# Half of the tokens runs four expert entries ahead of the other half, in all four layers

## The chip, the cores and the metric

The kernel runs on one core of one Trainium2 chip. The metric is the device time of one launch in microseconds (us); each kernel is judged by the median of its runs. Before the change the three runs took 655.57, 655.82 and 659.88 us.

## What is computed

Four layers, each of them an attention block and a mixture of experts, on 1024 tokens (4 batches of 256) of width 128, all in float32. Every block works on a layer-normed x, and its result is added to x with a gate of its own:

```python
x = x + tanh(g_xattn[L]) * attention_L(layernorm(x), ctx_1024)
x = x + tanh(g_ffn[L])   * experts_L(layernorm(x))
```

The attentions have 16 heads of 8. Layer 0 weighs rolled values by the top lags of a correlation taken over the head's 8 positions, layer 1 is plain softmax attention with biases, layer 2 a band of 32 positions to each side with one key head for all queries, layer 3 softmax attention under a 256 x 256 mask, with biases. The experts:

```python
# layer 0: 32 experts silu(x@g)*(x@u)@d of width 64 and 8 "zero" experts (x itself); softmax + bias, top 6
# layer 1: 16 of the same form, top 2 renormed, and one shared expert of width 352 with a sigmoid gate
# layer 2: 31 experts gelu(x@W1+B1)@W2+B2 of width 128, top 3; one shared expert; and + x
# layer 3:  8 experts relu(x@W1+b1)@W2+b2 of width 256, top 2
out = sum_e gate[token, e] * expert_e(x)
```

## The kernel before

All tokens stay in SBUF. Every large product is made of three TensorE matmuls, high x high, high x low and low x high parts of fp32r numbers (`product`, L731 to L736), on 128 rows and 512 columns, so the 1024 tokens are two halves of 512 (`hf` 0 and 1).

*Experts.* Every token goes through every expert, weighted by its gate, which is zero where the expert wasn't chosen. An entry is a 128-wide piece of expert weights: 16 entries in layer 0 (two experts of width 64 side by side), 11 in layer 1 (8 such pairs and 3 pieces of the shared expert), 32 in layer 2, 16 in layer 3. A *unit* is an entry on one half of the tokens, so a layer has twice as many units as entries; unit u is entry u // 2 on half u % 2. A unit runs through the engines like this:

- SyncE loads the entry's weights into one of four ring slots (`fill_ring` L357 before the stage, `load_ring` L364 in it) and, from the fourth entry on, the entry's row of gates, broadcast to 128 partitions, into `gate_slot` (held in `qst`).
- GpSimd splits the weights into high and low parts (`split_weights` L467: L475 gives the high part, L477 the low one; `hidden_part` L480 for the up weights, `result_part` L486 for the down weights), once an entry.
- TensorE makes the up product (L738; three matmuls in the MLP layers 2 and 3, six in the GLU layers 0 and 1), for the first three entries spreads the gate row itself (L754), and makes the down product (L768), which adds to a sum that stays in PSUM, one bank a half, for the whole stage. The up of a unit stands two units ahead of its down.
- ScalarE applies silu, gelu or relu (`unit` L1168) and later copies the weighted result to `hid_hi` (`first_part` L1178).
- VectorE multiplies with the gate (L1589; in GLU layers gate by up first, L1575) and subtracts for the low part `hid_lo` (L1595). In layers 0 and 2 it also adds the layer's own input, tile by tile (`add_input` L1552).

*Start of a stage.* `ln_turned` (DVE, L1369; L1374 is the low part `xlo` of the turned, normed tokens) ends a norm. Half 0's is done first; then come the norm of half 1 and `route` (PE L703, DVE L1476, ACT L1147), whose operations take all eight tiles of 128 tokens at once: scores, top k, renorm, and a three-way bf16 split of the table, which TensorE turns into rows (`turn_rows` L715, `turn_weights` L721). Only then do units' products with gates begin.

*End of a stage.* The two sums are scaled (ACT and DVE), turned back by eight transposes (L829), added to x, and the next norm and the attention's query product (`project_queries` L853, weights split at `split_query_weights` L509) follow. In these stretches TensorE multiplies zeros (`keep_busy` L569, L572) where it would idle.

*Attention.* A hand-written software pipeline over (batch, head) steps p (`loop` L1024 and L1239; `window_loop` L1051 for layer 2): maxima, scores, exponentials on ScalarE (L1273), values, norm of the outputs, with the second half's queries projected at steps `Q_AT`. Layer 3 makes 16 mask products (L848) ahead of the loop.

Each engine runs its own instruction list in the order that the code writes; semaphores join them. No planner is involved.

## Time and profile before

| | |
|---|---|
| median of three runs | 655.82 us |
| the profiled execution | 655.92 us, of which the span of the trace is 654.1 us |
| mean granted TensorE clock | 0.967 |
| TensorE matmul busy | 594.5 us (91%), 3429 instructions |
| VectorE busy | 502.1 us (77%) |
| ScalarE busy | 360.2 us (55%) |
| GpSimd busy | 222.0 us (34%) |
| layer 3's mask products (L848) | 4.1 us for 16 matmuls, which the trace shows as 32 records |
| expert stages, from half 0's `xlo` to the last down | about 41 to 135, 228 to 294, 364 to 472, 583 to 643 us |

A page of the profile has its times in us. Engines are PE (TensorE), PEld (its weight loads), DVE (VectorE), ACT (ScalarE), POOL (GpSimd) and SP (SyncE, SPq its DMA issues). A matmul record is the time from its start to the end that is modelled for it; the next one starts before it ends, so a row of 0.39 us and the next start 0.23 us later go together. "[idle before <-X]" is the idle time ahead of an instruction and who ended it. PEclk is the granted clock as a share of full speed.

### The profile page before, as it was taken

Reading aid. Unit: us, or ns where it says so; the run is one execution under the profiler, and the core shown is the slowest. Engines: PE = TensorE matmul, PEld = TensorE weight load, DVE = VectorE, ACT = ScalarE, POOL = GpSimd, SP = SyncE. Lnnn points to the kernel's source line nnn. Section 1 sums busy time; section 2 is a strip of 40 time slices with the busy share of each in tenths; the row PEclk is TensorE's granted clock in tenths of the full one; section 3 lists DMA queues with packets and bytes.
Section 4 is the critical chain, followed back from the end, with each engine's and each line's share of the span. In section 5 each row is a group of like instructions: output and inputs, shape, how many; then the busy total and the mean of one; then the engine's idle time right before and its main releaser. Section 6 shows DMA issues by size and latency. Waiting matters only on the chain.

```text
span 654.1 us, 11738 instructions
## 1 busy us (share of the span) xinstructions
PE 594.5 (91%) x3429; PEld 433.6 (66%) x3429; DVE 502.1 (77%) x1287; ACT 360.2 (55%) x639; POOL 222.0 (34%) x438
## 2 busy tenths in 40 slices
PE   8898699978999878997999799999998999987996
PEld 6684588746776555874666556888865777754784
DVE  7857779978777357997753579999968888655996
ACT  6326345525666514553566157888824666632885
POOL 4211255432000212532112126888831000201783
PEclk9989889998999979999999899999997999998999
DMA  8225886210000005811000217777410000000771
GB/s 289 66 97 152 181 196 176 76 50 1 4 28 3 27 1 122 195 35 33 4 6 18 57 50 251 237 241 234 153 33 2 3 28 3 4 2 10 263 243 42
DMA packets 33134, 59.06 MB, mean 90 GB/s; under 512 B 6530, under 2 KB 22562, under 8 KB 33084
## 3 DMA queue, kind: packets, MB, share of 16 engines
q1 hardware_dynamic: 32508, 57.43, 30.1%
q10 hardware_dynamic: 576, 1.02, 0.4%
q8 instruction: 25, 0.41, 0.2%
q14 instruction: 25, 0.20, 0.1%
HBM read 53.61 MB, written 4.29 MB: 89 GB/s over the span
## 4 chain that ended last, share of the span: by engine, by line
PE 69%; DVE 16%; ACT 5%; issue 5%; SPq 3%; DMA 2%; POOL 1%; DVEq 0%; ACTq 0%
PE PS L734 11%; PE PS L736 10%; PE PS L735 10%; PE PS L983 5%; PE PS L891 4%; PE PS L966 4%; PE PS L572 2%; PE PS L963 2%; PE PS L1000 2%; DVE hid_lo L1595 2%; ACT pT L1273 2%; PE PS L939 1%; DVE qst L1649 1%; DVE PS L1589 1%; PE PS L920 1%
## 5 line engine op out<-in xcount | busy, mean ns | idle before, releaser
L475 POOL TENSOR_TENSOR wpair<-ring,ones_col 128x128 fp32r<-128x128 f32 (+1 forms) x150 | 80.0, 533 | 149.0 <-PE PS L736 125.0
L1273 ACT ACTIVATE pT<-PS 128x512 f32<-128x512 f32 x160 | 92.6, 595 | 46.0 <-PE PS L966 37.6
L1595 DVE TENSOR_TENSOR hid_lo<-PS,hid_hi 128x512 fp32r<-128x512 f32 x150 | 102.4, 682 | 1.8 <-ACT hid_hi L1182 1.3
L1182 ACT ACTIVATE hid_hi<-PS 128x512 fp32r<-128x512 f32 x150 | 88.9, 593 | 19.0 <-DVE PS L1589 18.5
L477 POOL TENSOR_TENSOR wpair<-ring,wpair 128x128 fp32r<-128x128 f32 (+1 forms) x150 | 93.2, 621 | 11.8
L734 PE MATMUL PS<-xhi,wpair 128*128 128x512 f32 x204 | 85.0, 417 | 6.0 <-POOL wpair L477 4.9
L735 PE MATMUL PS<-xlo,wpair 128*128 128x512 f32 x204 | 82.5, 404 | 0.0
L736 PE MATMUL PS<-xhi,wpair 128*128 128x512 f32 x204 | 82.3, 404 | 0.0
L1176 ACT ACTIVATE pT<-PS,ring 128x512 f32<-128x512 f32 x96 | 65.9, 689 | 17.6 <-PE PS L736 16.3
L734 PE MATMUL PS<-hid_hi,wpair 128*128 128x512 f32 x150 | 62.1, 414 | 6.8 <-DVE hid_lo L1595 6.4
L966 PE MATMUL PS<-qst,kz 128*128 128x256 f32 x256 | 64.6, 338 | 3.0 <-ACT pT L1273 3.0
L1589 DVE TENSOR_TENSOR PS<-pT,qst 128x512 f32<-128x512 f32 x84 | 62.8, 748 | 5.3 <-ACT pT L1176 2.3
L891 PE MATMUL PS<-kz,qst 128*128 128x256 f32 x256 | 60.6, 321 | 4.8 <-DVE negmax L1696 2.6
L532 POOL CAST nmpart<-negmax 128x8 fp32r<-128x8 f32 x48 | 9.1, 189 | 157.7 <-DVE emask L1703 67.3
L1696 DVE CUSTOM_DVE_ANT_0 consts<-PS,ctx_tok,negfloor 128x256 bf16<-128x256 f32 x128 | 54.6, 481 | 8.1 <-PE PS L891 7.8
L736 PE MATMUL PS<-hid_hi,wpair 128*128 128x512 f32 x150 | 58.9, 393 | 0.0
L735 PE MATMUL PS<-hid_lo,wpair 128*128 128x512 f32 x150 | 58.9, 393 | 0.0
L1176 ACT ACTIVATE pT<-PS 128x512 f32<-128x512 f32 x54 | 32.1, 598 | 48.4 <-PE PS L736 48.3
L1690 DVE TENSOR_REDUCE negmax<-PS 128x2 f32<-128x512 f32 x64 | 42.0, 688 | 15.8 <-PE PS L891 15.7
L891 PEld LDWEIGHTS PS<-kz,qst 128*128 128x128 f32 x256 | 40.5, 197 | 17.9 <-issue 6.9
L734 PEld LDWEIGHTS PS<-xhi,wpair 128*128 128x128 f32 x204 | 40.2, 197 | 16.9 <-POOL wpair L477 5.3
L966 PEld LDWEIGHTS PS<-qst,kz 128*128 128x128 f32 x256 | 45.6, 196 | 7.3 <-issue 2.8
(239 smaller groups left out, 1118.0 us busy)
## 6 DMA issues: line engine op xcount, KB each, us to landing
qst<-gates SPq DMA_DIRECT2D x42, 512.0 KB, 4.8
qst<-gates SPq DMA_DIRECT2D x42, 256.0 KB, 4.3
ring<-in_mlp SPq DMA_DIRECT2D x48, 128.5 KB, 3.3
ring<-in_glu SPq DMA_DIRECT2D x27, 192.0 KB, 4.6
kz<-keys SPq DMA_DIRECT2D x36, 96.0 KB
keys<-qst SPq DMA_DIRECT2D x6, 512.0 KB, 3.6
qst<-kfull SPq DMA_DIRECT2D x96, 4.0 KB
wq<-in_wq SPq DMA_DIRECT2D x3, 256.0 KB, 3.6
```

The lines of the kernel that those rows point to most:

```text
L475: pool.tensor_tensor(wpair[:, pair, 0, c], w, ones, ALU.mult).then_inc(M["wstep"], 1)
L477: pool.tensor_tensor(wpair[:, pair, 1, c], ring[:, slot, c], wpair[:, pair, 0, c].bitcast(f32), ALU.subtract).then_inc(ready, 1)
L734: pe.matmul(o, w_hi, hi, start=start, stop=False, skip_group_check=True)
L735: pe.matmul(o, w_hi, lo, start=False, stop=False, skip_group_check=True)
L736: return pe.matmul(o, w_lo, hi, start=False, stop=start, skip_group_check=True)
L891: mm = pe.matmul(PS[:, v % 2, q * S:(q + 1) * S], qst[:, h // HGRP, b * S + q * P:b * S + (q + 1) * P], keys_of(b, h), start=True, stop=True)
L966: mm = pe.matmul(PS[:, 2 + w % 2, k * S:(k + 1) * S], keys_of(b, h)[:, k * P:(k + 1) * P], qst[:, h // HGRP, b * S:(b + 1) * S], start=(L ...
L1176: act.activation(act_out[:, hf if glu else kept, :], PS[:, 2 + hf, :], func, bias=bias).then_inc(M["act"], 1)
L1182: act.activation(hid_hi[:, kept, :], PS[:, gate_bank(glu, kept), :], ACT.Copy).then_inc(M["hi"], 1)
L1273: act.activation(pT[:, w % 8, :], PS[:, 2 + w % 2, :], ACT.Exp, scale=sc).then_inc(A["p"], 1)
L1589: dve.tensor_tensor(o, src, row, ALU.mult).then_inc(M["hid"], 1)
L1595: dve.tensor_tensor(hid_lo[:, kept, :], PS[:, gate_bank(glu, kept), :], hid_hi[:, kept, :].bitcast(f32), ALU.subtract).then_inc(M["lo"], 1)
```

## The change

1. *Order of the units.* Half 0 runs four entries ahead: the first four units are entries 0 to 3 of half 0, then the halves alternate, half 1 four entries behind, and the last four units are half 1 alone. For these last four, entries 0 to 3 are read from memory and split a second time. "Step" s is an entry as it is loaded: s runs to n + 3, and s >= n are the second readings. An up now stands up to four units ahead of its down in layers 2 and 3.
2. *Routing.* Each half is scored and routed by itself; half 0's at the start of the stage, half 1's add, norm and routing between units 0 to 5. The table is turned as one f32 matrix, and its rows are kept as a high and a low part (`high_rows`, `low_rows`) with K = 64 in place of three bf16 parts with K = 96. Rows are saved and loaded from entry 6 on (unit 8).
3. *Ends.* Half 0's sum is complete four units before the end; it is turned back, added and normed between the last units, so attention begins with half 0's queries right behind the last down. The next layer's query weights are split in four pieces at steps 9 to 12 (layer 2: at steps n to n + 3). In layer 3 each half is added and stored by itself. The zero matmuls around the stages (16 and 6 at the ends, 13, 22 and 10 at the starts, 8 before a stage) are gone.
4. *Attention.* Half 1's turn back, add and norm stand inside the loop (steps 8 to 18 of layers 1 and 3, 0 to 7 of layer 2), its queries at steps 20 to 26. Two key chunks move from layer 0's experts into layer 1's loop; layer 3's mask products go into its loop. The output bias becomes a TensorE product with a row of ones, in place of additions on GpSimd.
5. *Smaller ones.* Layer 0's input is added by GpSimd (`add_tokens`), layer 2's by TensorE with a unit matrix. From unit 8 on, the MLP layers' activation is written to its PSUM bank, and multiplied by the gate in place. SyncE's order in layer 0 is ring slots 0 and 1, keys, slots 2 and 3, then the rest, with three key stacks at steps 12 to 14.

The core of the diff:

```diff
+AHEAD = RING
+BY_PE = 2 * AHEAD
+FIRST_ROW = AHEAD + 2
...
+        def unit_at(L, u):
+
+            n = ROUTE[L]["ENT"]
+            if u < AHEAD:
+                s, hf = u, 0
+            elif u < 2 * n - AHEAD:
+                s, hf = (u + AHEAD) // 2, u % 2
+            else:
+                s, hf = u - n + AHEAD, 1
+            return u, s, hf, u % KEPT, s % 2
...
-                def save_gates():
-                    sp.wait_ge(rows_out, L + 1)
-                    for j in range(4):
-                        sp.dma_start(gd[L].rearrange("e (a j n) -> j e a n", a=NHALF, j=4)[j],
-                                     gate_rows[EP * j:EP * (j + 1), :].rearrange("e (a n) -> e a n", a=NHALF)).then_inc(rows_saved, 16)
...
+                def save_gates(hf):
+                    sp.wait_ge(rows_out, NHALF * L + hf + 1)
+                    sp.dma_start(gd[L][:, hf * HALF:(hf + 1) * HALF], gate_rows[:, hf, :]).then_inc(rows_saved, 16)
+
+                def both_parts(s):
+                    e = s if s < n else s - n
+                    ring_part(s, e, s % RING)
+                    row_part(s, e, s % RING, half=(s >= n))
...
-                    save_keys(3)
-                    stack_keys(1, range(KSLOTS))
-                    save_gates()
-                    save_keys(2)
-                    shift_windows()
...
+                for s in range(n if L == 2 else 3 * RING, n + AHEAD):
+                    both_parts(s)
+                    if L == 0 and s < 3 * RING + KSLOTS:
+                        stack_keys(1, (s - 3 * RING,))
```

On GpSimd and TensorE, the new code of the ends and starts reads:

```python
                for s in range(2 * RING if L == 2 else n + AHEAD):   # GpSimd
                    if s + 1 < n + AHEAD:
                        hidden_part(s + 1)
                    else:
                        if L < 3:
                            layer_norm(2 * L + 2, (0,))
                    result_part(s)
...
                def step(u):                                         # TensorE
                    if u < 2 * n - 5:
                        up(*U(u + 4))
                    down(*U(u))
                    if u == 2 * n - 5:
                        turn_back(L, 0)
                        up(*U(u + 4))
                    if u == 2 * n - 2 and L < 3:
                        layer_norm(2 * L + 2, (0,))
```

VectorE at the start of layer 2's experts, before: the end of the routing of all eight tiles, the copy of the turned weights (L1550), and the first product with a gate (L1589). `pT` is the workspace of routing and activations, `PS` is PSUM.

```order
L1508 MATCH_REPLACE pT<-top,pT 128x31 x8
L1513 TENSOR_REDUCE rsum<-pT 128x8
L1514 RECIPROCAL rrec<-rsum 128x8
L1515 SCALAR_TENSOR_TENSOR pT<-pT 128x8x31
L1532 TENSOR_TENSOR pT<-pT,rrec 128x8x31
L1534 MEMSET pT 128x8
L1541 CAST pT<-pT 128x8x32
L1543 TENSOR_TENSOR pT<-pT 128x256
L1544 CAST pT<-pT 128x8x32
L1545 TENSOR_TENSOR pT<-pT 128x8x32
L1550 COPY pT<-PS 96x512
L1589 TENSOR_TENSOR PS<-pT,PS 128x512
```

The same place after the change: half 0's routing, then half 1's sum (L1604) and moments (L1574 to L1579), half 0's low rows (L1760), and the first two products with a gate (L1782).

```order
L1720 MATCH_REPLACE pT<-top,pT 128x31 x4
L1725 TENSOR_REDUCE rsum<-pT 128x4
L1726 RECIPROCAL rrec<-rsum 128x4
L1727 SCALAR_TENSOR_TENSOR pT<-pT 128x4x31
L1744 MEMSET pT 128x4
L1745 TENSOR_TENSOR pT<-pT,rrec 128x4x31
L1604 SCALAR_TENSOR_TENSOR x_res<-PS,gtan,x_res 128x512
L1574 BN_STATS stats<-x_res 128x6 x4
L1760 TENSOR_TENSOR wqpair<-PS,wqpair 32x512
L1577 BN_AGGR mv<-stats 128x2 x4
L1579 TENSOR_SCALAR veps<-mv 128x4
L1782 TENSOR_TENSOR PS<-oT,PS 128x512 x2
```

The routing has 4 tiles where it had 8, the four operations of the three-way split (L1541 to L1545) and the copy are gone, and the second half's norm now stands around the first products, not ahead of the routing.

TensorE at the end of layer 2's experts, before: the last down (L734 to L736), the transposes of both halves (L829), 16 zero matmuls, layer 3's mask products (L848), the norm's transposes (L582), six more zero matmuls, the first query product (L862).

```order
L734 MATMUL PS<-hid_hi,wpair 128x512
L735 MATMUL PS<-hid_lo,wpair 128x512
L736 MATMUL PS<-hid_hi,wpair 128x512
L829 MATMUL PS<-consts,oT 128x128 x8
L572 MATMUL PS<-zerob 128x512 x16
L848 MATMUL PS<-vall,ctx_tok 128x144 x16
L582 MATMUL PS<-consts,xn 128x128 x4
L572 MATMUL PS<-zerob 128x512 x6
L862 MATMUL PS<-xhi,wqpair 128x512
```

After: the last downs of half 1, with half 0's normed tokens transposed between them (L638), and the query product (L972) right behind.

```order
L791 MATMUL PS<-hid_hi,wpair 128x512
L792 MATMUL PS<-hid_lo,wpair 128x512
L793 MATMUL PS<-hid_hi,wpair 128x512
L638 MATMUL PS<-consts,xn 128x128 x4
L791 MATMUL PS<-hid_hi,wpair 128x512
L792 MATMUL PS<-hid_lo,wpair 128x512
L793 MATMUL PS<-hid_hi,wpair 128x512
L972 MATMUL PS<-xhi,wqpair 128x512
L973 MATMUL PS<-xlo,wqpair 128x512
L974 MATMUL PS<-xhi,wqpair 128x512
L977 MATMUL PS<-ones,brow 128x512
```

Zero matmuls, mask products and both halves' turn back have left the stretch between the last down and the query product; half 0's turn back stands four units earlier.

## Rows read from the trace of the kernel before

**Rows 1.** Windows: us; busy us (x instructions) of PE, PEld, DVE, ACT, POOL; PEclk; DMA; GB/s.
```profile
405.00:450.00 45.00, 45.00 (x199) 36.67 (x198) 43.07 (x67) 38.56 (x67) 39.96 (x66) 1.00 0.74 239
366.80:373.45 6.65, 3.21 (x20) 1.75 (x19) 3.98 (x15) 0.60 (x1) 1.01 (x1) 0.88 0.00 0
375.35:382.85 7.50, 7.50 (x28) 3.83 (x28) 6.88 (x38) 1.89 (x3) 1.66 (x4) 0.78 0.01 2
239.20:247.10 7.90, 7.37 (x28) 4.56 (x28) 7.22 (x40) 2.31 (x5) 2.15 (x4) 0.81 0.00 0
46.50:56.80 10.30, 9.85 (x24) 5.12 (x23) 9.03 (x41) 5.54 (x9) 2.15 (x4) 0.78 0.08 30
```
**Rows 2.** Timeline, DVE, starts of stages: start us, duration us, line, operation [idle before].
```profile
40.71 0.69 DVE L1374 TENSOR_TENSOR xlo<-PS,xhi 128x512 fp32r<-128x512 f32 x1 [0.42 <-ACT xhi L1111]
...
69.86 0.69 DVE L1589 TENSOR_TENSOR PS<-pT,PS 128x512 f32<-128x512 f32 x1
...
227.95 0.69 DVE L1374 TENSOR_TENSOR xlo<-PS,xhi 128x512 fp32r<-128x512 f32 x1 [0.43 <-ACT xhi L1111]
...
258.27 0.69 DVE L1589 TENSOR_TENSOR PS<-pT,PS 128x512 f32<-128x512 f32 x1
...
364.31 0.69 DVE L1374 TENSOR_TENSOR xlo<-PS,xhi 128x512 fp32r<-128x512 f32 x1 [0.40 <-ACT xhi L1111]
...
393.69 0.70 DVE L1589 TENSOR_TENSOR PS<-pT,PS 128x512 f32<-128x512 f32 x1
...
474.63 0.70 DVE L1589 TENSOR_TENSOR PS<-pT,qst 128x512 f32<-128x512 f32 x1
...
583.30 0.68 DVE L1374 TENSOR_TENSOR xlo<-PS,xhi 128x512 fp32r<-128x512 f32 x1
...
609.26 0.69 DVE L1589 TENSOR_TENSOR PS<-pT,PS 128x512 f32<-128x512 f32 x1 [0.33 <-ACT pT L1176]
```
**Rows 3.** Timeline, PE and SP queue, ends of the expert stages.
```profile
131.88 0.39 PE L734 MATMUL PS<-hid_hi,wpair 128*128 128x512 f32 x1
...
146.14 0.50 PE L862 MATMUL PS<-xhi,wqpair 128*128 128x512 f32 x1
...
292.11 0.39 PE L734 MATMUL PS<-hid_hi,wpair 128*128 128x512 f32 x1
...
304.73 0.50 PE L862 MATMUL PS<-xhi,wqpair 128*128 128x512 f32 x1
...
469.63 0.39 PE L734 MATMUL PS<-hid_hi,wpair 128*128 128x512 f32 x1
...
488.88 0.50 PE L862 MATMUL PS<-xhi,wqpair 128*128 128x512 f32 x1
...
640.15 0.39 PE L734 MATMUL PS<-hid_hi,wpair 128*128 128x512 f32 x1
...
651.08 0.35 SPq L449 DMA_DIRECT2D out_x<-x_res  x1
```
**Rows 4.** Waits of PE: us in total, times, longest us.
```profile
PE PS L734 <- POOL wpair L477: 4.9, 1, 4.9
```
**Rows 5.** Page, DMA issues: operation, count, KB each, us from issue to landing.
```profile
qst<-gates SPq DMA_DIRECT2D x42, 256.0 KB, 4.3
```
**Rows 6.** Groups by form, then the timeline, of POOL's splits and a DVE product.
```profile
L475 POOL TENSOR_TENSOR wpair<-ring,ones_col 128x128 fp32r<-128x128 f32 x123 | 63.4, 516 | 81.8 <-PE PS L736 77.8 <-DMA ring<-in_mlp 2.9
...
L477 POOL TENSOR_TENSOR wpair<-ring,wpair 128x128 fp32r<-128x128 f32 x123 | 72.8, 592 | 9.6
...
L477 POOL TENSOR_TENSOR wpair<-ring,wpair 128x256 fp32r<-128x256 f32 x27 | 20.4, 755 | 2.1
...
465.12 0.90 DVE L1589 TENSOR_TENSOR PS<-pT,qst 128x512 f32<-128x512 f32 x1
...
465.54 0.79 POOL L477 TENSOR_TENSOR wpair<-ring,wpair 128x128 fp32r<-128x128 f32 x1
...
640.74 0.46 POOL L477 TENSOR_TENSOR wpair<-ring,wpair 128x128 fp32r<-128x128 f32 x1
```

1208 lines of the change are left out of this document (721 added, 487 removed).

## Prediction

> **What bounds the kernel now.** I read the core's span and clock first, then the windows, the timeline around each change of stage, and the groups by form. The span is 654.1 us, the profiled execution 655.92 us, so 1.8 us lie around the span; the median of the three runs is 655.82 us, which is the same, and sums below are made against 655.9.
>
> In the middle of an expert stage nothing but TensorE matters: from 405 to 450 us it is busy 45.00 of 45.00 us at full clock, while VectorE has 43.07, ScalarE 38.56 and GpSimd 39.96 [rows 1]. Its 199 matmuls there are 0.226 us each, so I take 1.37 us for the six of an MLP unit and 2.04 us for the nine of a GLU unit. The change leaves these matmuls alone, so no gain lies there.
>
> The time lies between the stages. Entering the experts of layer 2, the low part of the first half's tokens starts at 364.31, and unit 5's product with its gate at 393.69 [rows 2]. In between TensorE waits or multiplies zeros, while VectorE does the second half's norm (3.98 us busy of 6.65) and then the routing of all 8 tiles (6.88 of 7.50) [rows 1]. The other way, the last steps of the expert stage and the first query product are 19 us apart [rows 3]. Layer 0 has a hole of its own: TensorE waits 4.9 us for split weights whose load came late [rows 4].
>
> **Part 1: the starts of the expert stages.** The first half is now routed alone. I count from the half-0 xlo to a fixed unit, as VectorE's work, because that engine carries norm, routing and units. Scoring starts 2.0 us after xlo starts (0.7 for it, then two or three fillers and the eight router matmuls). Routing one half costs half of the old busy time less the 1.4 us of the removed three-way split, and a floor, since small operations don't halve: 5.0 us in layer 0 (old 9.03), 4.2 in layer 1 (7.22), 3.0 in layer 2 (6.88) [rows 1], and as much in layer 3. A norm of a half is 4.0, a low-row or hidden product 0.69 [rows 1, 2].
> Layer 2, up to hid of unit 5: 3.0 + 4.0 + 0.7 + five hid and five lo (6.9) + 3.0 + 0.7 = 18.3, with 0.5 for waits 18.8; 364.3 + 2.0 + 18.8 = 385.1 against 393.69: 8.6 us.
> Layer 3 the same: 583.3 + 2.0 + 18.8 = 604.1 against 609.26: 5.2 us.
> Layer 1, up to hid of unit 4, with three operations a unit that start some 0.63 apart: 4.2 + 4.0 + 0.7 + 8.3 + 4.2 = 21.4, then 0.7 for low rows behind it: 227.95 + 2.0 + 22.1 = 252.0 against 258.27: 6.3 us.
> Layer 0: 5.0 + 1.8 (apply and xlo) + 5.0 + 1.4 + 8.7 + 1.0 of waits = 22.9; 40.71 + 1.9 + 22.9 = 65.5 against 69.86: 4.4 us [rows 2].
> Together 24.5. From this I take 4.0: in layers 2 and 3 unit 8 is the first with a loaded gate row, rows are saved only after the second half is routed, and save plus load take some 6 us (a load by the gates lands in 4.3 us [rows 5], a save I take at 2) against three units of 1.37 us: 2 us late, twice. I add 1.4: the eight additions of the input leave VectorE in layer 2, where VectorE held back the first units (unit 5 at 393.69, unit 63 at 474.63 [rows 2], which is 1.4 us more than 58 x 1.37). Result +21.9. Bounds: 12 (VectorE's inserted steps each wait about 1 us for TensorE and ScalarE) to 26.
>
> **Part 2: the hole of layer 0.** From hid of unit 4 (69.86) to the end of up 27 are 53.8 us: down 28 starts at 131.88 [rows 3], and four ups and five downs without a stall (8.9 us) before its end give 123.7. At 2.04 a unit it would be 46.2, so 7.6 us are stalls. The new order of SyncE's queue sends ring slots before key copies, so they should go. But three key stacks (0.4 MB each) now fall into entries 12 to 14 and four entries are loaded twice, and the DMA engines are well filled by such loads (0.74 busy in the middle of layer 2 [rows 1]): I leave 3.0. Result +4.6, bounds 0 to 7.6.
>
> **Part 3: the ends.** Entries 0 to 3 are loaded and split a second time, so GpSimd must split a whole entry per unit, not per two. A pair of 128-column splits is 0.95 us undisturbed (means 516 and 592 ns, and 0.46 us for the second where nothing disturbs it), a 256-column pair 1.4 (the second 755 ns, the first in proportion) [rows 6]; the square root of the norm 1.0, GpSimd's one operation in the second row of [rows 1]. What is queued behind the waiting instruction is everything: TensorE's next up stands ahead of its next down.
> MLP, counted from the end of down 2n-7: result split 1.0, query split 0.6, hidden split 1.0, up 0.7, two downs 1.4 (4.6); result, query, hidden 2.5, up 0.7 (7.8); down, result, query split 2.3, rstd 1.0, apply 1.1, transposes, xhi and xlo 2.0, 14.2 in all. One more up is done by then (0.7) and 0.5 is lost just before, so 14.0 against 488.88 - 470.32 = 18.6 in layer 2 (470.32 is the end of the down that starts at 469.63) [rows 3]: +4.6. This count contains the mask products that leave the path (16 matmuls, 4.1 us in the table of the profile).
> GLU, from the end of up 2n-5: 5.15 to up 2n-2, 7.7 after its down, splits to 10.1, up and down 12.2, split and rstd 14.1, apply 1.1, then the last unit's chain on VectorE and ScalarE 3.4 and xlo 0.7: 19.3. Old: 146.14 - 123.7 = 22.5 in layer 0, 304.73 - 283.9 = 20.8 in layer 1 (where query splits add 1.0) [rows 3]: +3.2 and +0.5.
> Layer 3 has no next stage: 12.5 us from the end of down 2n-7 to the issue of the last store against 651.08 - 640.83 = 10.25 (the down starts at 640.15) [rows 3]: -2.3.
> Result +6.0, bounds -8 to +16.
>
> **Part 4: the start of attention.** The second half's norm (4.0 us) moves into the loop. In layers 1 and 3 it stands at steps 9 to 18, where ScalarE's exponentials set the pace; it costs nothing while that cover holds. In layer 2 it stands at steps 1 to 7, where VectorE sets the pace: -2.5 of 4.0. In layer 1 two key chunks, in layer 3 the mask products stand among the first steps, and TensorE waits there for a ScalarE that has just turned to exponentials: -2.5 and -1.5. Result -6.5, bounds 0 to -12.
>
> **Part 5: the clock.** At the starts TensorE was granted 0.78 to 0.88 of full clock after its waits [rows 1]: half speed for some microseconds. The fillers are gone, so it will fall again, mostly under VectorE's work: -2.0, bounds 0 to -8.
>
> Fifty-odd fewer filler matmuls and the biases that GpSimd added to x cost nothing before, being hidden by the norm, and give nothing. Sum: 21.9 + 4.6 + 6.0 - 6.5 - 2.0 = 24.0, so 655.9 - 24.0 = **632 us**.
>
> **A rule weighed.** In layer 2 GpSimd is close to its limit, and the solo entries ask for more. In the trace a split that overlaps VectorE's product of two SBUF tiles takes 0.79 us, and the product 0.90, while the same split has 0.46 elsewhere [rows 6]. The change writes the activation into PSUM, so that product reads one tile of SBUF. The Trainium skill, SBUF — State Buffer, section "Who interferes with whom", says that a DVE instruction with two SBUF inputs contends with a GpSimd instruction that reads SBUF, and one with a single SBUF input does not. By that rule four splits fall to about 2.0 us against 2.73 for two units; without it they stay at 2.4 to 2.7. The trace agrees as far as it goes. The sum above rests on 0.95 for a pair; with 1.3 part 3 would lose 3 us.
>
> **Rivals.**
> A, late transfers: layer 0's hole stays whole (4.6 back) and the first loaded rows of layers 2 and 3 come 5 us late each, not 2 (6 more): 643. For it: the loads already take 0.74 of the DMA engines' time. Against: the ring is four entries deep.
> B, the overlap is given back: TensorE runs at half clock (0.2 us more for each matmul) through the first five solo units of each stage; 9 x 0.2 x 5 = 9 us in each of two GLU stages and 6 in each MLP stage, 30 in all, of which VectorE's own work hides about 10: 632 + 20 = 652, no measurable difference. For it: the clock of 0.78 and 0.81 in the routing windows [rows 1]. Against: VectorE is the slower there.
> C, slower: GpSimd becomes the bound of layers 2 and 3. If the new accesses contend as the worst pair above on all four splits, an entry takes 3.8 us, not 2.73; the 28 and 12 entries after the solo ones give 43 us and the solo ones 10 more: 685. It decides from 3.3 us for four splits, where the loss equals the gain. Against it: 0.46 us beside products that read PSUM.
> D, better: loads keep up (+3), the loop absorbs what I charge it (+6), GpSimd is a step ahead in the tails (+6): 617.
>
> **How the numbers follow.** Forecast 0.55, A 0.18, B 0.07, C 0.05, D 0.15. Faster by over 1% (which is about what a measurement of this kernel tells from no change) are forecast, A and D: 0.88; within 1% is B: 0.07; slower C: 0.05. The range reaches down almost to D and past A: 619 to 647.
>
> **What would show it.** Right: unit 5 of layer 2's experts 20 to 22 us behind its xlo, not 29; loops again at 1.37 and 2.04 us a unit; TensorE waits for splits of 1 to 2 us only in the last four units; no hole near 75 us. Wrong: a unit pitch above 1.45 us in layer 2 (C or a slow ScalarE), long waits for gate rows (A), a clock below 0.8 over 10 us at a start (B), or first scores of attention no earlier after the last unit than before.

## The result

The changed kernel takes 697.4 us, median of four runs (693.6 to 711.3), against 656.3 us: 1.060 times as long, 95% interval 1.053 to 1.066. 632 us were forecast. The ratio and its interval leave out the run of 711.3 us, in which the granted clock was 0.915 where the other three had 0.943 to 0.952. Run once more beside later kernels it took 699.7 us (ratio 1.068). In its profiled execution the span is 691.8 us, 37.7 more than before.

From the page of the changed kernel: span, busy time of the engines, and the chain that ended last by engine.

```profile
span 691.8 us, 11249 instructions
...
PE 591.5 (86%) x3299; PEld 432.4 (63%) x3299; DVE 494.1 (71%) x1296; ACT 373.2 (54%) x662; POOL 227.6 (33%) x532
...
PE 65%; DVE 13%; ACT 6%; POOL 5%; DMA 5%; issue 5%; SPq 1%; ACTq 0%; POOLq 0%; DVEq 0%
```

TensorE's busy time is 3 us less than before; its idle time is 41 us more. The useful work is nearly the same, and 134 products with zeros are gone (189 records before, 55 now); the busy time hardly fell for it, and more of what is left ran at half speed, as the last part of this section shows. GpSimd and DMA, together 3% of the last chain before, are 10%.

I cut the span at the same events in both kernels: the first half's `xlo` at each start (DVE L1596, was L1374), the product with a gate that [rows 2] show (L1782, was L1589; unit 4 in layers 0 and 1, unit 5 in layers 2 and 3), an event four or more units before the end, and the first query product (PE L972) or the store. First the starts:

```profile
39.46 0.69 DVE L1596 TENSOR_TENSOR xlo<-PS,xhi 128x512 fp32r<-128x512 f32 x1 [0.42 <-ACT xhi L1231]
...
72.51 0.69 DVE L1782 TENSOR_TENSOR PS<-pT,PS 128x512 f32<-128x512 f32 x1
...
234.53 0.69 DVE L1596 TENSOR_TENSOR xlo<-PS,xhi 128x512 fp32r<-128x512 f32 x1 [0.43 <-ACT xhi L1231]
...
262.54 0.69 DVE L1782 TENSOR_TENSOR PS<-pT,PS 128x512 f32<-128x512 f32 x1
...
379.60 0.69 DVE L1596 TENSOR_TENSOR xlo<-PS,xhi 128x512 fp32r<-128x512 f32 x1 [0.40 <-ACT xhi L1231]
...
407.41 0.70 DVE L1782 TENSOR_TENSOR PS<-oT,PS 128x512 f32<-128x512 f32 x1 [2.75 <-ACT oT L1303]
...
609.92 0.68 DVE L1596 TENSOR_TENSOR xlo<-PS,xhi 128x512 fp32r<-128x512 f32 x1
...
638.42 0.70 DVE L1782 TENSOR_TENSOR PS<-oT,PS 128x512 f32<-128x512 f32 x1 [1.22 <-ACT oT L1303]
```

They answer to [rows 2]. From `xlo` to the product: 33.1, 28.0, 27.8 and 28.5 us in layers 0 to 3; before 29.2, 30.3, 29.4 and 26.0. Then the ends, PE and SyncE's queue:

```profile
141.21 0.80 PE L972 MATMUL PS<-xhi,wqpair 128*128 128x512 f32 x1
...
315.53 0.79 PE L972 MATMUL PS<-xhi,wqpair 128*128 128x512 f32 x1
...
485.13 0.40 PE L793 MATMUL PS<-hid_hi,wpair 128*128 128x512 f32 x1
...
502.21 0.80 PE L972 MATMUL PS<-xhi,wqpair 128*128 128x512 f32 x1
...
689.33 0.34 SPq L498 DMA_DIRECT2D out_x<-x_res  x1
```

All but the third answer to [rows 3]; 485.13 is the last matmul of layer 2's down 57. With 0.23 us for it, 16.85 us run to the query product, 18.6 before.

| us, before minus after (plus is gained) | forecast | measured |
|---|---|---|
| up to the first `xlo` | 0 | +1.3 |
| starts, layers 0, 1, 2, 3 | 4.4, 6.3, 8.6, 5.2 | -3.9, +2.3, +1.6, -2.5 |
| between start and end, same layers | 4.6, 0, -0.6, -2 | +6.7, -4.8, -1.3, -5.1 |
| ends | 3.2, 0.5, 4.6, -2.3 | +0.9, -1.7, +1.8, -4.0 |
| attention, first query product to next `xlo`, layers 1, 2, 3 | -6.5 in all | -11.5, -4.5, -13.3 |
| the clock, apart | -2.0 | in the rows above |

In the GLU layers the end is counted from the low part of unit 2n - 7 (118.96 and 291.7 us, before 123.0 and 282.65), in layer 3 from down 25 to the store. With 0.5 us behind the store the column adds up to -37.5; the spans differ by 37.7.

Windows of the changed kernel (columns as in [rows 1]): a loop in layer 2's experts, the start of layer 2, pieces of the starts of layers 1 and 3, and steps 8 to 24 of layer 1's attention.

```profile
450.00:475.00 25.00, 25.00 (x112) 20.71 (x111) 23.32 (x38) 21.73 (x37) 15.72 (x38) 1.00 0.79 243
389.10:404.10 15.00, 12.28 (x47) 7.79 (x47) 11.35 (x37) 6.71 (x12) 6.17 (x15) 0.89 0.09 24
246.00:256.00 10.00, 9.85 (x29) 7.60 (x30) 5.57 (x15) 1.71 (x4) 2.16 (x4) 0.54 0.07 20
621.00:630.00 9.00, 8.98 (x25) 5.88 (x24) 3.65 (x12) 1.78 (x3) 2.80 (x7) 0.50 0.05 15
166.60:190.10 23.50, 18.66 (x155) 13.79 (x156) 13.32 (x22) 12.62 (x27) 1.58 (x8) 1.00 0.05 14
```

The loop is as it was, 0.22 us a matmul at full clock. In the second row VectorE is busy for 11.35 of 15 us, and in the third and fourth TensorE has work all the time at half speed (0.54, 0.50). The mean granted clock is 0.946 (before 0.967), so of the span 2 x 0.054 x 691.8 = 75 us were at 1.2 GHz, and 43 us before. What runs 32 us longer at half speed would take at least 16 us at full speed, so by this estimate the clock can account for at most 16 of the 37.7 us. The last row is to be held against the same 16 exponentials of the kernel before:

```profile
167.50:185.10 17.60, 16.77 (x150) 12.45 (x150) 12.21 (x21) 11.58 (x25) 1.57 (x8) 1.00 0.07 20
```

Five more matmuls, 6 us longer: TensorE is busy for 1.9 us more and idle for 4.0 us more. What TensorE waits for longest (in all, times, longest):

```profile
PE PS L791 <- POOL wpair L526: 23.2, 16, 3.2
PE PS L791 <- DVE hid_lo L1786: 13.4, 6, 4.1
PE PS L972 <- DVE qst L1918: 9.3, 6, 1.7
PE PS L638 <- DVE xn L1588: 7.7, 4, 2.6
```

Before, waits for split weights were 4.9 us [rows 4].

### The profile page after: what moved, and what is told of

Its sections match the earlier page's. It is cut to its first block, busy times and chain, and to the rows that moved or that the text cites. A ratio compares the mean times of both kernels' runs of the same rounds, so it can differ in the third digit from the quotient of the medians.

```text
span 691.8 us, 11249 instructions
## 1 busy us (share of the span) xinstructions
PE 591.5 (86%) x3299; PEld 432.4 (63%) x3299; DVE 494.1 (71%) x1296; ACT 373.2 (54%) x662; POOL 227.6 (33%) x532
## 4 chain that ended last, share of the span: by engine, by line
PE 65%; DVE 13%; ACT 6%; POOL 5%; DMA 5%; issue 5%; SPq 1%; ACTq 0%; POOLq 0%; DVEq 0%
PE PS L791 11%; PE PS L793 10%; PE PS L792 9%; PE PS L1087 5%; PE PS L995 4%; PE PS L1070 3%; POOL wpair L526 2%; DMA ring<-in_mlp 2%; POOL wpair L524 2%; PE PS L1104 2%; PE PS L1067 2%; DVE negmax L1976 2%; DVE consts L1982 1%; PE PS L638 1%; DVE qst L1918 1%
## 5 line engine op out<-in xcount | busy, mean ns | idle before, releaser
L1499 ACT ACTIVATE pT<-PS 128x512 f32<-128x512 f32 x160 | 92.8, 594 | 52.6 <-PE PS L1070 45.4
L791 PE MATMUL PS<-xhi,wpair 128*128 128x512 f32 x204 | 87.0, 426 | 23.2 <-POOL wpair L526 23.2
L1782 DVE TENSOR_TENSOR PS<-PS,qst 128x512 f32<-128x512 f32 x118 | 82.1, 695 | 13.0 <-ACT PS L1303 10.4
L793 PE MATMUL PS<-xhi,wpair 128*128 128x512 f32 x204 | 82.2, 403 | 0.0
L791 PE MATMUL PS<-hid_hi,wpair 128*128 128x512 f32 x150 | 63.9, 426 | 13.4 <-DVE hid_lo L1786 13.4
L1982 DVE CUSTOM_DVE_ANT_0 consts<-PS,ctx_tok,negfloor 128x256 bf16<-128x256 f32 x128 | 54.6, 479 | 17.3 <-PE PS L995 17.1
L791 PEld LDWEIGHTS PS<-xhi,wpair 128*128 128x128 f32 x204 | 40.2, 197 | 40.9 <-POOL wpair L526 29.9
L1303 ACT ACTIVATE PS<-PS,ring 128x512 f32<-128x512 f32 x80 | 53.0, 662 | 23.4 <-PE PS L793 22.7
L793 PE MATMUL PS<-hid_hi,wpair 128*128 128x512 f32 x150 | 61.8, 412 | 0.0
L792 PE MATMUL PS<-hid_lo,wpair 128*128 128x512 f32 x150 | 61.8, 412 | 0.0
L1303 ACT ACTIVATE kfull<-PS 128x512 f32<-128x512 f32 x54 | 32.2, 597 | 47.1 <-PE PS L793 47.1
L995 PEld LDWEIGHTS PS<-kz,qst 128*128 128x128 f32 x256 | 39.1, 191 | 22.5 <-issue 10.5
```

Of the source, the lines that this page charges most:

```text
L791: pe.matmul(o, w_hi, hi, start=start, stop=False, skip_group_check=True)
L792: pe.matmul(o, w_hi, lo, start=False, stop=False, skip_group_check=True)
L793: return pe.matmul(o, w_lo, hi, start=False, stop=start, skip_group_check=True)
L995: mm = pe.matmul(PS[:, v % 2, q * S:(q + 1) * S], qst[:, h // HGRP, b * S + q * P:b * S + (q + 1) * P], keys_of(b, h), start=True, stop=True)
L1303: act.activation(o, PS[:, 2 + kept % 2, :], func, bias=bias).then_inc(M["act"], 1)
L1499: act.activation(pT[:, w % 8, :], PS[:, 2 + w % 2, :], ACT.Exp, scale=sc).then_inc(A["p"], 1)
```

## The experiments

Single edits of a few us can't be read from the medians: the changed kernel gave 694 to 711 us. In the order in which they are told here, the medians were 699.7 (the changed kernel again), 703.2 and 699.4 (queries three and four apart), 704.4 (narrow norm), 703.5 and 702.9 (table first, narrow entry), 708.1, 701.7 and 708.5 (no tables, zero products, layer 0's order), 693.3 and 704.0 (narrow tail, early query splits) and 691.4 (four together). So each is read where it acts, from its profile: for attention from the stage's `xlo` to exponential 0, 8 and 24 of ScalarE, for expert stages from `xlo` to the low part of a unit. Below, "the changed kernel" stands for both of its profiles, which agree within 0.4 us in attention and 0.3 us in layer 2's experts; in layer 0's they differ by 2.5 us (101.0 and 103.5).

**1. The changed kernel again.**

> The changed kernel once more, unchanged, as the measure for the runs beside it on this chip. The four runs with small edits gave 701 to 708 us where the changed kernel had given 697, though their stages at the edited places got shorter: the granted clock was half of full for 76 to 116 us in them. Theory 'the gaps at the starts make the clock a matter of chance': this run too lies anywhere between 692 and 710, with 75 to 115 us at half clock, and its stages away from the starts agree with the first run within 0.5 us. Rival 'the edits made it worse': 697 or less and at most 80 us at half clock.

699.7 us; mean clock 0.945. Attention 93.8, 64.8, 108.4 us (94.1, 64.8, 108.5 in the first). Its 699.7 us and the 77 us at half speed in its profile lie in the theory's ranges, its stages away from the starts too, but for layer 0's. So the 701 to 708 us of the four edits run before it need not mean that they made the kernel worse: their profiles have mean clocks of 0.920 to 0.947, and 707.4 us came without any edit (clock 0.919). One place shows what the clock costs. Layer 2's start is the same code in ten of the profiles. Unit 9's low part comes 34.3 to 34.5 us behind `xlo` when the clock stays up, and 38.9 to 42.8 us when it falls (mean from `xlo` to there 0.95, against 0.68 to 0.79). The start of layer 2 in the run with queries four apart (experiment 2):

```profile
390.10:405.10 15.00, 12.62 (x32) 7.98 (x32) 7.87 (x21) 4.22 (x7) 4.91 (x11) 0.50 0.10 26
```

15 us at 0.50 throughout; the changed kernel has 0.89 in the same stretch (second window above). The kernel before is at 38.4 there.

**2. Query products further apart.**

```diff
-        Q_AT = (20, 22, 24, 26)
+        Q_AT = (19, 22, 25, 28)      # e1
+        Q_AT = (17, 21, 25, 29)      # e7, norm at 9, 10, 11, 13, 16 on VectorE, 15 on TensorE
```

(e1 is three apart, e7 four apart; e7 also moves layer 2's turned tokens from step 7 to 5.)

> The changed kernel with the second half's query products at loop steps 19, 22, 25, 28 in place of 20, 22, 24, 26 (layers 1 and 3). All four use PSUM bank 7, so each waits until VectorE has taken the one before; two steps apart TensorE stands still until that (six waits, 9.3 us, and the exponentials fall 6 us behind in layer 1 and 8 us in layer 3 over these steps). Theory 'queries in lockstep': the waits go, the attentions of layers 1 and 3 get 4 to 6 and 5 to 8 us shorter, in all 10 to 14 us. Rival 'the norm inside the loop costs it, or the clock does': under 3 us, since VectorE has the same work and the same number of waits on it.

> The changed kernel with the second half's query products four steps apart (17, 21, 25, 29, as far apart as in the kernel before) and its norm one or two steps earlier. Two apart, steps 8 to 24 of the exponentials took 23.5 us in layer 1 and 27.2 in layer 3; three apart 22.2 and 25.1; before, sixteen steps with the four products in them took 18 to 20. Theory 'one bank, in order': four apart TensorE never waits for VectorE to have taken the last query; steps 8 to 24 take 20.5 to 21.5 us in layer 1 and 23.5 to 24.5 in layer 3. Rival 'the products themselves cost it': no shorter than three apart, within 0.3 us.

The changed kernel's pattern, with four products and three such waits in each of two loops: VectorE takes the query, and only then does TensorE write the next into the same bank.

```profile
171.15 0.74 DVE L1918 SCALAR_TENSOR_TENSOR qst<-PS,consts,qst 128x512 fp32r<-128x512 f32 x1
...
171.94 0.50 PE L972 MATMUL PS<-xhi,wqpair 128*128 128x512 f32 x1 [1.44 <-DVE qst L1918]
```

| us | before | 2 apart | 3 apart | 4 apart |
|---|---|---|---|---|
| layer 1, exponentials 0 to 24 | 26.5 | 32.5 | 31.1 | 30.1 |
| layer 1, 8 to 24 | 17.4 | 23.5 | 22.1 | 18.5 |
| layer 3, 0 to 24 | 29.3 | 37.8 | 35.7 | 34.0 |
| layer 3, 8 to 24 | 19.6 | 27.2 | 25.1 | 20.7 |

Three apart the waits shrink from 9.3 us to

```profile
PE PS L972 <- DVE qst L1918: 3.5, 4, 1.0
```

and four apart they leave the list. Part of the drop from 8 to 24 is that one product moved ahead of step 8; over 0 to 24 spacing gives 2.4 and 3.8 us of the 5.9 and 8.4 lost. The mechanism is shown; its size was overestimated: 10 to 14 us were expected of three apart, 3.5 came. Of the rest only a part is added work. From exponential 0 to 24 TensorE's records fill 25.3 of 26.5 us before and 25.8 of 30.1 four apart in layer 1, 29.1 of 29.3 and 30.3 of 34.0 in layer 3: 0.5 and 1.2 us more busy, 3.1 and 3.4 us more idle. In the kernel before TensorE has next to no idle time there, so a wait put into the loop is paid for too. Which waits make up what is left was not tested.

**3. VectorE's norm inside the loop, made small** (the second half's columns are mostly left out). The addition, which runs on 512 columns in the changed kernel; statistics, apply and low part are made narrow likewise:

```diff
+                            link(dve.tensor_tensor(x[:, 4, 0:8], PS[:, 7, 0:8], x[:, 4, 0:8], ALU.add))
```

> The changed kernel with the second half's add, statistics, apply and low part inside the loops of layers 1 and 3 done on 8 columns instead of 512 or 128 (so the second half's queries are wrong there): some 3 us less of VectorE in each loop, every wait and every TensorE instruction as it was. The exponentials fell 2.5 us behind between steps 8 and 12 in each. Theory 'VectorE's inserts stop TensorE': TensorE's scores alternate between two PSUM banks, so it waits when VectorE is a step late; these 2.5 us go, 2 to 3 in each layer. Rival 'it is the added TensorE products and ScalarE's copy': at most 0.7 us in each.

Counted from the stage's `xlo`, exponential 16 comes at 41.5 us in layer 1 (41.6 to 41.9) and 48.0 in layer 3 (48.6 to 48.7). But this run reached exponential 0 later, 1 us in layer 1, where its clock had been 0.79 and not 0.94. In the changed kernel the norm lies between exponentials 0 and 8 (its `xlo` at 166.37, exponential 0 at 157.62), and there 8.9 us became 7.8 in layer 1 and 10.6 became 9.6 in layer 3; a run that entered layer 1 at a low clock and kept its norm took 8.6. From 8 to 16 nothing changed. So the norm costs about 1 us in each loop: less than the theory's 2 to 3, more than the rival's 0.7, and neither holds as it was put. The slip between 8 and 12 that I took for the norm stays without it; it is where the query products stand.

**4. The entry of attention.**

```diff
+                act.activation(warm[:, 2:3], gates[:, 0:1], ACT.Exp).then_inc(astep, 1)
                 for a in range(HGRP):
                     take_queries(0, a, 2 + a)
-                act.activation(warm[:, 2:3], gates[:, 0:1], ACT.Exp).then_inc(astep, 1)
```

> The changed kernel with ScalarE's load of the exponential table moved ahead of the four query copies at each attention's start. In the changed kernel layer 1's key chunk (TensorE waits 3.4 and 2.6 us for its high part) and layer 3's mask products wait behind the copies and the table load. Theory 'the entry waits for ScalarE in order': the load then runs while TensorE makes the first queries, and the entries of layers 1 and 3 get 1 to 1.3 us shorter each, layer 2 0 to 1, 2 to 4 in all. Rival 'it only moves the wait to the query copies': 0, or 1 to 2 us slower.

The second kernel narrows what was moved into the first steps; layer 2's keys and layer 3's mask part are left out but for a few columns.

```diff
-                            mm = pe.matmul(PS[:, 7, q * H * 9:(q + 1) * H * 9],
-                                           maskedT[:, k, q * P:(q + 1) * P], vall[3][:, TB * b + k, :, :],
+                            mm = pe.matmul(PS[:, 7, q * H * 9:q * H * 9 + 9],
+                                           maskedT[:, k, q * P:(q + 1) * P], vall[3][:, TB * b + k, 0, :],
...
+                c = 8 if n >= KV_LN + 2 else HALF
```

> The changed kernel with the pieces that entered the first steps of the attention loops made small: layer 1's two key chunks copied by ScalarE on 8 columns instead of 512, layer 3's mask products on 9 columns of 144 (the keys of layer 2 and the mask's part of layer 3 are then wrong). From the first xlo to the first exponential the changed kernel takes 17.1 us in layer 1 (13.0 before) and 20.3 in layer 3 (15.6 before). Theory 'the pieces moved into the loop are the entry's loss': layer 1 1 to 2 us and layer 3 2 to 3.5 us shorter; what then is left above before is the wait for ScalarE's table and order. Rival 'only the waits between engines count, not the sizes': under 0.7 us in each.

Table first: exponential 0 at 15.7, 20.1 and 17.5 us (17.1, 19.3 and 20.3; before 13.0, 16.1, 15.6). In layer 1 that is 1.1 to 1.4 us earlier than in runs at the same clock (0.95), of which by exponential 16 at most 0.4 is left; in layer 2 it is 0.8 later. In layer 3 most of the 2.8 us is the clock: three runs without this edit that kept 0.95 to 1.00 there have 18.1 to 18.5 us, so 0.5 to 1 us is the edit's.

Small pieces: 19.4 and 21.6 us, later than the changed kernel, but at a clock of 0.68 and 0.67 where that had 0.94 and 0.84. Layer 1's entry in the run with early query splits (experiment 6), which has the pieces whole, and in this one, each from `xlo` to exponential 0:

```profile
143.72:163.59 19.87, 17.08 (x58) 10.72 (x57) 10.55 (x16) 8.28 (x13) 0.79 (x4) 0.67 0.13 41
143.50:162.86 19.36, 16.98 (x58) 10.66 (x57) 10.55 (x16) 6.61 (x14) 0.78 (x4) 0.68 0.13 42
```

At like clock small pieces gain 0.5 us, as the rival has it. For layer 3 no other run entered at such a clock, so the size of the mask products stays untested there. Of the 4.1 and 4.7 us that the entries of layers 1 and 3 lost, the order on ScalarE explains about 1 us each; the rest is open.

**5. The starts: tables, zero products, order.**

```diff
-                    first_use(ACT.Exp)
                     exponentials(1, 1)          # computed as silu; in layer 2, edited likewise, as gelu
                     high(3)
-                    first_use(func)
```

> The changed kernel with the second half's routing exponentials of layers 1 and 2 computed by the stage's own function (silu, gelu), so ScalarE loads no table between the first units: two loads of 1.28 us less in each of two layers; the second half's gates are then not softmax values. Theory 'the second half's routing chain holds everything': in layer 2 no activation runs from 396.5 to 406.7 us, two table loads stand in that chain, so the start gets 2.6 us shorter in each, 5 in all, and not more, because the chain score, exponential, choice, turn, high, low, rows is still in order. Rival 'tables hidden behind VectorE': under 1 us. Rival 'tables are the chain': 8 us or more.

The second half's gates are not softmax values there. ScalarE in layer 2's start of the changed kernel:

```profile
396.52 0.69 ACT L1303 ACTIVATE oT<-PS,ring 128x512 f32<-128x512 f32 x1 [2.88 <-PE PS L793]
...
397.71 1.28 ACT L1276 ACT_TABLE_LOAD   x1
...
399.59 0.30 ACT L1271 ACTIVATE pT<-pT 128x124 f32<-128x124 f32 x1
...
403.37 0.59 ACT L1284 ACTIVATE wqpair<-PS 32x512 fp32r<-32x512 f32 x1 [2.99 <-PE PS L774]
404.70 0.59 ACT L1288 ACTIVATE pT<-PS 32x512 f32<-32x512 f32 x1 [0.74 <-DVE wqpair L1760]
405.30 1.28 ACT L1276 ACT_TABLE_LOAD   x1
...
406.71 0.67 ACT L1303 ACTIVATE oT<-PS,ring 128x512 f32<-128x512 f32 x1
```

Between two activations (L1303) lie 10 us: a table load, the exponential of the scores (L1271), the waits for TensorE's turned gates and for VectorE's low rows, and a second table load. Unit 5 is half 1's and needs all of it. Without the loads unit 5's low part comes at 32.1 us where the six other runs at low clock have 33.7 to 34.6 (layer 2), and at 33.3 against 33.8 in layer 1: some 2 and 0.5 us of 2.6 each. At unit 9 of layer 2 it has 39.0 us, no better than the best of those six (38.9). The chain is longer than the tables.

```diff
+                if L > 0:
+                    keep_busy(0, (0, 14, 6, 3)[L])
                 turn_rows(L, 0)
...
                     for u in (0, 1, 2):
+                        if L > 0:
+                            add_zeros(4)
...
+                    add_zeros(6)
                     down(*U(2))
                     up(*U(5))
                     up(*U(6))
+                    add_zeros(4)
```

> The changed kernel with zero products back at the starts of the expert stages of layers 1 to 3 (14, 6, 3 ahead of the first half's turned gates; 12 in layer 1 and 10 each in layers 2 and 3 between the first units, adding zeros to the first half's sum). The granted clock was half of full for 75 us of the changed kernel's run against 41 us before. Rival 'the clock is the loss': most of these 34 us go, and the time falls by 12 us or more. Theory 'order of the work': the clock at these three starts rises (10 to 15 us less at half), but the chain on ScalarE and VectorE stays, so 3 to 6 us.

701.7 us, with the mean clock at 0.947. Layer 3's start is 2.8 us shorter at unit 5 (27.1 for 29.9), layer 2's the same, layer 1's 4 us longer (37.8 for 33.8): there 14 zero products stand in order ahead of the turned gates, and unit 0's low part is already 2.8 us later. In layer 3 at unit 9 it has 35.9 us, and three runs that kept the clock up without zero products have 33.0 to 33.3. The run gained nothing on the whole, but it does not decide the rival "the clock is the loss": the time at half speed was 74 us for 75, gained at these starts and lost at the ends. What bounds the rival is the estimate of 16 us above, and that the loops of attention are slower at a clock of 1.00.

```diff
-                    turn_rows(0, 1)
...
                     spread(*U(1))
                     start_sum(0)
+                    if L == 0:
+                        turn_rows(0, 1)
...
                     low_rows(0)
-                    choose(0, 1)
                     gated(0, 0, True)
                     hid_of(0)
+                    choose(0, 1)
```

The first part is TensorE's list, the last VectorE's; ScalarE's stays as it was.

> The changed kernel with one piece of order mended in layer 0's start: VectorE makes unit 0's two products ahead of the second half's choice of experts, and TensorE spreads units 0 and 1 ahead of turning the second half's gates. In the changed kernel the first half's rows are there at 53.9 us and the first spread runs at 60.7, behind the second half's scores, choice and turned rows; unit 0's low part is 24.7 us behind the stage's first xlo, against 21.5 in the kernel before. Theory 'in order behind the second half': unit 0 comes 2 to 3.5 us earlier, units 4 and 5 1 to 3, since the choice (3.5 us of VectorE) then lies under TensorE's ups and downs. Rival 'ScalarE's copies of keys and its table load hold unit 0': under 1 us at unit 0 and nothing at unit 5.

Unit 0's low part went from 24.7 us (24.5 to 26.1 in the other runs) to 29.7. TensorE's spread waits for ScalarE's key copies, the rival's point; and with the choice now behind the product, ScalarE's list holds the second half's rows ahead of unit 0's high part:

```profile
60.38 0.76 PE L822 MATMUL PS<-wqpair,pick 64*128 64x512 f32 x1 [2.79 <-ACT qst L1247]
...
66.82 0.59 ACT L1285 ACTIVATE wqpair<-PS 32x512 fp32r<-32x512 f32 x1 [6.20 <-PE PS L774]
...
68.65 0.57 ACT L1314 ACTIVATE hid_hi<-PS 128x512 fp32r<-128x512 f32 x1
```

ScalarE waits 6.2 us for the turned gates, and `hid_hi` of unit 0, whose input had been ready since 61.96, follows at 68.65. Moving the order of two engines and leaving the third's lost 4 to 5 us at unit 0.

**6. The last units.**

```diff
-  split(max(2 * s, 1), s % RING, s % 2, slice(0, ups), M["wup"])
+  split(max(2 * s, 1), s % RING, s % 2, slice(0, 8 if s >= n else ups), M["wup"])
```

(and likewise for the down weights; the last four units' weights are left out but for 8 columns)

> The changed kernel with GpSimd's splits of the second readings (the last four units' weights, all layers) done on 8 columns instead of 128 or 256, so the last four units use stale weights. TensorE waits 16 times and 23 us in all for a split. Theory 'GpSimd bounds the last four units': from the fifth last unit to the next stage's first turned tokens the stages get 4 to 6 us shorter in layers 2 and 3 and 2 to 5 in layers 0 and 1, 12 to 20 in all. Rival 'the norm between the units and the clock bound them': under 6 us in all.

```diff
-                with pool.Fori(2, n // RING) as i:
+                with pool.Fori(2, n // RING - 1) as i:
...
-                    for s in range(n, n + AHEAD):
+                    for s in range(n - AHEAD, n + AHEAD):
...
-                        split_query_weights(3, s - n)
+                        if s < n:
+                            split_query_weights(3, s - n + AHEAD)
```

> The changed kernel with layer 3's four query splits on GpSimd at steps 28 to 31 of layer 2's experts (the last loop pass written out) in place of steps 32 to 35, where they stand between the splits that TensorE waits for. A pair takes 0.8 us. Theory 'GpSimd's queue is the path of the last units': two or three of the four are on it, so layer 2's last five units up to the next turned tokens (17.6 us) get 1.6 to 2.4 us shorter, and the loop stays at 1.37 us a unit. Rival 'the norm bounds it': under 0.5 us; or the pairs now cost the loop 1 us or more.

GpSimd in layer 2's end of the changed kernel, and TensorE's up 62 behind it:

```profile
485.61 0.40 POOL L524 TENSOR_TENSOR wpair<-ring,ones_col 128x128 fp32r<-128x128 f32 x1 [1.80 <-PE PS L793]
486.09 0.46 POOL L526 TENSOR_TENSOR wpair<-ring,wpair 128x128 fp32r<-128x128 f32 x1
486.49 0.29 POOL L587 CAST wqpair<-wq 128x128 fp32r<-128x128 f32 x1
486.86 0.45 POOL L589 TENSOR_TENSOR wqpair<-wq,wqpair 128x128 fp32r<-128x128 f32 x1
487.27 0.40 POOL L524 TENSOR_TENSOR wpair<-ring,ones_col 128x128 fp32r<-128x128 f32 x1
487.75 0.45 POOL L526 TENSOR_TENSOR wpair<-ring,wpair 128x128 fp32r<-128x128 f32 x1
...
488.26 0.50 PE L791 MATMUL PS<-xhi,wpair 128*128 128x512 f32 x1 [2.73 <-POOL wpair L526]
```

Result split, query split and hidden split stand in a row as the forecast has them, 0.85 + 0.8 + 0.85 us, and TensorE waits 2.73. With narrow splits the last units up to the next `xlo` (from unit 27, 17, 59, 27) take 12.0, 13.0, 15.4 and 15.2 us for 14.7, 16.3, 17.6 and 18.2 (17.3 in the second profile): 10 to 11 us in all, where I had said 12 to 20 for the theory and under 6 for the rival. The waits of the whole run that are left on these two engines (23.2 and 13.4 us before the edit) are hops between engines and, on GpSimd, the query splits, which this edit leaves whole:

```profile
PE PS L791 <- POOL wpair L526: 15.0, 13, 3.1
PE PS L791 <- DVE hid_lo L1786: 13.0, 13, 2.2
```

Even with free splits layer 3's end is longer than before (12.4 us). Layer 3's query splits taken to steps 28 to 31: layer 2's end takes 15.0 us for 17.6, 2.6 less, and the loop keeps its pace (1.36 us a unit). About 1 us of that is the clock, 1.00 in this end and 0.89 in the changed kernel's: the four mendings of experiment 7 have the same edit at 0.89 and take 15.9 us. They were on the path, for some 1.7 us.

**7. Four mendings together**: the edits of experiments 2 (four apart), 4 (table first), 5 (zero products) and 6 (query splits), but without the zero products of layer 1, those among its first units included:

```diff
-                    keep_busy(0, (0, 14, 6, 3)[L])
+                    keep_busy(0, (0, 0, 6, 3)[L])
```

> The changed kernel with four of the edits together: second half's queries four steps apart, exponential table first at each attention's start, zero products at the starts of layers 2 and 3 only (6 and 3 before the turned gates, 10 among the first units), layer 3's query splits at steps 28 to 31. If the costs add: queries 2.5 and 3.5, tables 1 to 2, splits 2, clock 4 to 8 at the two starts: 12 to 18 us less than the changed kernel on this chip, 682 to 688. If they only move waits to the next engine: 690 or more. Either way it stays slower than the kernel before, because the chains at the starts and ends stay.

691.4 us (690.6 to 694.3), ratio 1.054, against 699.7. Attention 90.9, 65.9 and 101.4 us for 93.8, 64.8 and 108.4; layer 2's experts 120.6 for 122.1; layer 1's 83.5 for 80.1, where nothing had been edited and the clock was lower (0.75 for 0.85 in its end). 8 us of the 12 to 18 came, and 691.4 lies in the second case as it was put (690 or more): part of what each edit gave alone did not add up.

**8. One part alone, on the kernel before: ring loads ahead of the rows.**

```diff
                     save_gates()
+                    ring_part(RING, 0, 0)            # b1 and b2: entry 4
                     save_keys(2)
                     shift_windows()
+                    ring_part(RING + 1, 1, 1)        # b2: entry 5; b2's mask loads go behind entry 7
```

> The kernel before, with one thing of the change alone: in layer 0 SyncE loads entry 4 into ring slot 0 right after it has saved the gates, ahead of the key copies, window shifts and mask loads (it was issued at 73.45 us, though slot 0 had been split since 53.5). Theory 'the hole is a late issue': TensorE's wait of 4.9 us near 75 us goes, or shrinks to under 1.5; the run gets 3.5 to 5 us shorter, 651 to 652.5. Rival 'the transfer is late anyway, the key copies take the DMA engines': 0 to 1.5 us.

> The kernel before with the loads of entries 4 and 5 of layer 0 both ahead of the first rows of gates, and the two mask loads behind entry 7. With entry 4 alone early, TensorE's wait of 4.9 us went and one of 3.8 us came, for entry 5: it was issued at 77.16 behind four row loads and landed at 85.4. Theory 'each load waits behind the rows': both waits go, layer 0's experts are 4 to 5 us shorter than in the kernel before, 651 to 652.5 in all. Rival 'now the rows are late': a wait for gate rows of 2 us or more takes their place, under 2 us gained.

Entry 4 alone: 655.8 us against 657.4, ratio 0.997 (0.995 to 1.000), not the 3.5 to 5 us of the theory. The wait of [rows 4] is gone and entry 5's stands in its place, GpSimd on the transfer and TensorE on the split:

```profile
85.45 0.61 POOL L484 TENSOR_TENSOR wpair<-ring,ones_col 128x256 fp32r<-128x256 f32 x1 [9.30 <-DMA ring<-in_glu]
...
87.00 0.49 PE L743 MATMUL PS<-xhi,wpair 128*128 128x512 f32 x1 [3.80 <-POOL wpair L486]
```

Both: **652.1 us** (648.8 to 654.3) against 656.6, ratio 0.993 (0.990 to 0.995). It is 4.5 us faster than the kernel before. SyncE issues entry 4, the key copies, entry 5, then six row loads:

```profile
66.78 0.59 SPq L393 DMA_DIRECT2D ring<-in_glu  x1
...
71.40 0.62 SPq L393 DMA_DIRECT2D ring<-in_glu  x1
...
72.13 0.55 SPq L374 DMA_DIRECT2D qst<-gates  x1
```

TensorE has no wait for a split left there, layer 0's experts take 99.0 us for 104.7. The two mask loads moved too, so their share of this is not told apart. In the changed kernel the same fault was cured in layer 0 and planted in layer 1, where the rows of steps 6 to 9 go ahead of the ring loads for 8 and 9:

```profile
279.15 0.61 POOL L524 TENSOR_TENSOR wpair<-ring,ones_col 128x256 fp32r<-128x256 f32 x1 [6.39 <-DMA ring<-in_glu]
...
280.62 0.50 PE L791 MATMUL PS<-xhi,wpair 128*128 128x512 f32 x1 [2.11 <-POOL wpair L526]
```

## Why the prediction was wrong

- **Which engine paces attention** (part 4: "where ScalarE's exponentials set the pace; it costs nothing while that cover holds"). This step failed most: -29.3 us for -6.5. It is TensorE that has no room in the loops of layers 1 and 3: before, it is busy for 25.3 of 26.5 and 29.1 of 29.3 us from exponential 0 to 24, while ScalarE has 17.3 and 18.9. The loops lost 5.9 and 8.4 us there (layer 2's 1.2). Shown of this are the query products two steps apart in one bank (2.4 and 3.8 us by spacing alone), which stood in no term of the sum, and the norm, which I had at nothing in these two loops (about 1 us each). The rest, 2.5 and 3.6 us, is open; turned tokens, key chunks and mask products are what else was put in. The entries come 4.1, 3.2 and 4.7 us later after the turned tokens; I had 2.5 and 1.5 us for layers 1 and 3 as a wait for ScalarE, and experiment 4 finds about 1 us of that kind in each.
- **Starts counted as VectorE's busy time** (part 1: "3.0 + 4.0 + 0.7 + ..."). -2.5 us for +24.5 (with the two corrections of part 1 the forecast was +21.9, bounds 12 to 26). The half's routing is a chain over four engines, each in order: score, exponential, choice, turn, high, low, rows; halving its width doesn't shorten its hops. That is read from the timeline; of its links only the table loads were tested. In layer 2 unit 5 came 27.8 us behind `xlo`, not 21. ScalarE's two table loads (1.28 us each) were in no term. In layer 0 the first half isn't routed ahead at all: its units stand behind the second half's choice, which the order of instructions would have told.
- **The clock** (part 5, -2.0; rival B). 75 us at half speed for 43. In layer 2 a start at half speed is 4.5 to 8.4 us longer, in layer 3 3 to 5 us (unit 9 at 33.0 to 33.3 us or at 36.6 to 38.3). My "mostly under VectorE's work" was wrong: the chain has TensorE's steps in it. At full speed the starts of layers 2 and 3 gain 4 and 0.8 us at unit 9, so rival B explains the sign of the starts of layer 3, not the size of the miss. By the estimate above it is at most 16 us in the whole run. The prediction also counts "fifty-odd fewer filler matmuls"; 134 are gone.
- **Layer 0's hole** (part 2, +4.6). Right, measured +6.7. Rival A's mechanism, late transfers, came in layer 1 (6.4 us on GpSimd, 2.1 on TensorE) and added to the -4.8 there; the rest of it was not traced. Layer 3's -5.1 for -2 in the same row of the table has 1.5 us of waits for splits and a clock of 0.92 in these 36.7 us, where the kernel before had 1.00.
- **The ends** (part 3, +6.0 within -8 to +16). -3.0. GpSimd's order was read rightly; 14.0 us in layer 2 became 16.85. The count has the splits that experiment 6 found on the path, and two things are missing in it: part of the last matmuls ran at half speed (records of 0.63 us for 0.40), worth about 1 us, and in the timeline ScalarE's copy of the sum, which waits for down 59, holds the next unit's high part. The second was not tested.
- **The rule weighed.** GpSimd's splits of the changed kernel by form:

```profile
L526 POOL TENSOR_TENSOR wpair<-ring,wpair 128x128 fp32r<-128x128 f32 x147 | 67.8, 461 | 11.5
...
L524 POOL TENSOR_TENSOR wpair<-ring,ones_col 128x128 fp32r<-128x128 f32 x147 | 59.2, 403 | 143.0 <-PE PS L793 119.4 <-DVE pT L1752 10.2 <-DVE pT L1745 8.4
```

  516 and 592 ns became 403 and 461 [rows 6], so four splits are 1.7 us where I took 2.0 by the rule. The Trainium skill's rule (SBUF — State Buffer, "Who interferes with whom") is borne out: beside products that read one tile of SBUF and take 0.70 us, not 0.90, the splits have the 0.46 us that [rows 6] show for one that nothing disturbs. Rival C, GpSimd as the loop's bound, did not happen; its sign came from elsewhere.

All the cases I had ended at 685 us or below, and four of five were gains, because each took the same sum and varied one term.

## What to carry over

When work is moved under a loop, first ask which engine the loop leaves no room, by its busy time in that window, and price the move in that engine's instructions, in the waits that it gets, and in the single buffers they share. A stage that is split in two halves keeps its hops: count the start as a chain through every in-order list, table loads included, not as the busy time of the engine with most work. A load that opens a stage belongs ahead of anything long on its queue, and the next one too. When the clock differs between two profiles of a kernel, compare a stage only with the same stage at the same clock: experiments 3 and 4 read otherwise without that.

## What the runs showed of the hardware

- The granted clock of the same instructions differs from run to run in the changed kernel, whose TensorE is idle for 100 us and not 60: mean 0.920 to 0.947 in the profiles of it and its variants, with stretches of up to 20 us at 1.2 GHz, and 694 to 711 us for one program. The kernel before keeps to 655 to 660 us, with clocks of 0.958 to 0.969.
- Loading a function table takes 1.28 us of ScalarE, and going from silu or gelu to the routing's exponential and back takes two of them, in each of layers 1 and 2.
- GpSimd's two split operations are 0.40 and 0.46 us beside VectorE products with one SBUF input, and 0.52 and 0.59 on average in the kernel before.
